# A decoder layer on one core: the softmax maximum moves into a spare row of the queries, and the transposed mask becomes one matmul per pair of heads

## The chip, the core and the metric

The kernel runs on one core of one Trainium2 chip. The metric is the device time of one execution in microseconds (us), the median of several runs. The core has five engines that run their own instruction streams and meet at semaphores: TensorE (PE in the profile), VectorE (DVE), ScalarE (ACT), GpSimd (POOL) and SyncE (SP), which here only issues transfers.

## The reference, cut to what matters

The layer takes x of 16 x 256 tokens with 128 features. It adds a selective-scan mixer, then a cross attention to 64 context keys per batch row, then a mixture of 8 experts with the best two chosen per token. The change is in the cross attention alone:

```
qh, kh, vh = heads of (q @ w_q.T + b_q), (k @ w_k.T + b_k), (v @ w_v.T + b_v)   # 16 heads of 8
score = einsum('bhqd,bhkd->bhqk', qh, kh) / sqrt(8)
score = where(mask == 0, -1e9, score)          # mask depends on query and key alone
attn  = softmax(score, axis=-1)                # subtracts each row's maximum
out   = einsum('bhqk,bhkd->bhqd', attn, vh) @ w_o.T + b_o
```

## The kernel before, in words

Two batch rows (512 tokens) are one unit of work; there are 8. The main loop has 8 rounds of 16 steps. In round r, step k, `body(r, k)` does one piece of the scan of unit r, and puts pieces of three other jobs between: the start of the mixer of units r+1 and r+2, the attention of unit r-1, and the end of the attention and the routing of unit r-2. What stands in which step is written out by hand in each engine's `slot` function, and each engine runs its list in that order. After the rounds, `drain` gives the attention of units 6 and 7 out between the 39 groups of the expert stage.

The scan in one step. ACT makes four decay tiles (`decays`, L1203) for the step three ahead, once VectorE's scan four steps back is done. DVE multiplies (`inputs`, L1711) and scans (`scan`, L1720). POOL multiplies (L1508) and folds (L1513) the states. PE sums them (`sum_states`, tile Y). The tiles lie in rings of four.

The attention of a unit has two passes over the scores. In the first (`scores`), queries lie on the partitions, and DVE takes each head's maximum over the 64 keys (`maxima`, L1737, steps 11 to 13). `split_max` (L1739) then makes minus the maximum as a sum of three bf16 numbers with five small DVE instructions. PE turns them (`turn_max`, L792), ACT copies them out of PSUM in one instruction (`copy_max`, L1254). In the second pass (`scores_t`, L798) keys lie on the partitions. To each product of keys and queries one bf16 matmul per pair of heads adds minus the maximum (`selmax` times `nmT`), and two more add the mask (`mbias2` times `identb`). ACT takes the exponential (`exps`, L1258).

Keys and queries are stored so that a contraction over 64 partitions serves one half of the heads. `qT` has two copies of the queries, w = 0 and 1, each with half of the 8-row head blocks set to zero (`queries`, L1119, by `qscale`). `Kbd` holds the keys four times, each with one head block kept in each group of 32 rows (`key_blocks`, L1243: four ACT instructions that scale `KT` by a column).

Three hand-overs stand near the change. `copy_xh` (ACT, L1207) at step 15 fills a PSUM tile that `steps_x` (DVE, L1693) multiplies at once. In step 6 ACT has one long block: `copy_kv`, `spreads`, `copy_xh`, `key_blocks`, `att_square`, `silus`, `att_inverse_root` (its last instruction is L1117). `att_normed` (DVE, L1732, step 9) needs the result of that last one.

## Time and profile before

| what | value |
|---|---|
| median of 3 runs | 830.47 us (830.2 to 832.67) |
| profiled execution: time / span | 829.18 / 827.4 us |
| busy: PE / DVE / ACT / POOL | 685.5 / 683.8 / 522.6 / 619.2 us |
| instructions: PE / DVE / ACT / POOL | 3923 / 1041 / 1223 / 467 |
| rounds of the scan | about 26 to 600 us of the span |
| `scores_t` pass, bf16 matmuls: `nmT,selmax` / `identb,mbias` | 128 / 256 |
| `Kbd` instructions on ACT | 32 |

The profiled execution took 829.18 us, of which the span, from its first to its last instruction, is 827.4. Busy time is summed per engine. A row of the timeline gives start and duration in us, the engine, the source line, the output and input tiles, the count of merged instructions, and in brackets how long the engine stood idle before and who released it. A row of `PE L649` is any matmul made through the helper at L649, so its tiles say which it is. The end of one instruction may overlap the start of the next on the same engine by about 0.1 us.

### The profile page before, as it was taken

To read this page: it belongs to the slowest core of one execution; us is meant where nothing else is said; L and a number is where in the kernel's file an instruction comes from. 1 tells how busy PE (TensorE), PEld (TensorE's weight loads), DVE (VectorE), ACT (ScalarE), POOL (GpSimd) and SP (SyncE) were. 2 spreads that over 40 slices of the span, in tenths; PEclk is the share of its full clock that TensorE was granted. 3 is DMA by queue.
4 is the path that set the end of the run, shared out by engine and by line. 5 is a ranking of instruction groups with operands and counts; after the bars stand their busy time and mean duration, and the time that the engine had idled before them with its cause. 6 is when DMAs were issued, how large, how long until landed. Compare 5 with 4: busy or idle time off the path is not lost. (4 is left out here: it accounts for less than half of the span.)

```text
span 827.4 us, 12371 instructions
## 1 busy us (share of the span) xinstructions
PE 685.5 (83%) x3923; PEld 477.2 (58%) x3923; DVE 683.8 (83%) x1041; ACT 522.6 (63%) x1223; POOL 619.2 (75%) x467
## 2 busy tenths in 40 slices
PE   6578759897898888889898798874778899899991
PEld 3453426555565555556555455552557678899981
DVE  3679999999999999999999999999953555865673
ACT  4687847787966977796697789567124334333353
POOL 1359988878899999999999999899752254675542
PEclk9679678999999999999999999989799999999997
DMA  4536595454538646534734644376064344886773
GB/s 106 205 116 163 183 280 183 127 202 161 156 125 225 211 152 199 169 130 128 228 136 154 190 158 154 109 237 211 27 211 127 97 139 128 268 294 219 230 257 102
DMA packets 80411, 142.70 MB, mean 172 GB/s; under 512 B 10555, under 2 KB 53574, under 8 KB 80346
## 3 DMA queue, kind: packets, MB, share of 16 engines
q1 hardware_dynamic: 75802, 133.38, 51.5%
q0 software_dynamic: 4544, 8.54, 2.9%
q8 instruction: 31, 0.51, 0.3%
q14 instruction: 34, 0.28, 0.1%
HBM read 110.25 MB, written 37.27 MB: 178 GB/s over the span
## 5 line engine op out<-in xcount | busy, mean ns | idle before, releaser
L1508 POOL TENSOR_TENSOR prod<-hst,BC 128x1024 f32<-128x1024 f32 x128 | 301.0, 2360 | 48.6 <-DVE hst L1720 40.0
L1720 DVE TENSOR_TENSOR_SCAN hst<-dA,Rp 128x1024 f32<-128x1024 f32 x128 | 292.3, 2284 | 9.0 <-ACT dA L1203 0.4
L1203 ACT ACTIVATE dA<-dtm,Aneg 128x255 f32<-128x255 f32 x512 | 213.9, 495 | 52.6 <-DVE hst L1720 52.0
L1513 POOL TENSOR_TENSOR prod<-prod 128x512 f32<-128x512 f32 x128 | 161.3, 1270 | 2.4
L1711 DVE TENSOR_TENSOR Rp<-BC,Rp 128x1024 f32<-128x1024 f32 x128 | 156.9, 1226 | 6.0 <-DMA BC<-bcd 0.6
L1628 POOL DMA_INDIRECT y2d<-prod,back x78 | 77.2, 990 | 101.6 <-DVE prod L2091 85.4
L649 PE MATMUL Y<-prod,ident 128*128 128x256 f32 x512 | 141.3, 409 | 14.3 <-POOL prod L1513 12.2
L649 PEld LDWEIGHTS Y<-prod,ident 128*128 128x128 f32 x512 | 101.4, 206 | 52.1 <-issue 19.1
L649 PE MATMUL Mb<-hpad,winT 128*128 128x512 f32 (+1 forms) x176 | 79.6, 598 | 14.5 <-ACT xh L1152 11.9
L649 PEld LDWEIGHTS Rp<-BC,xh 128*128 128x128 f32 x624 | 75.3, 192 | 7.7 <-ACT xh L1449 4.1
L649 PE MATMUL Rp<-BC,xh 128*128 128x128 f32 x624 | 76.4, 276 | 3.5 <-ACT xh L1449 3.5
L1552 POOL DMA_INDIRECT xsd<-x2o,slots x64 | 63.2, 987 | 17.5 <-issue 16.6
L649 PE MATMUL T<-Kbd,qT 64*128 64x256 f32 x256 | 50.2, 447 | 22.8 <-DVE mx L1737 19.7
L1442 ACT ACTIVATE soft<-Y 128x256 f32<-128x256 f32 x37 | 14.2, 384 | 83.9 <-PE Y L1045 83.9
L649 PEld LDWEIGHTS Mb<-hpad,winT 128*128 128x128 f32 x176 | 34.7, 205 | 51.5 <-issue 25.5
L649 PEld LDWEIGHTS T<-Kbd,qT 64*128 64x128 f32 x256 | 30.3, 204 | 41.7 <-DVE mx L1737 29.1
L1262 ACT ACTIVATE E<-T 128x512 f32<-128x512 f32 x64 | 34.7, 594 | 30.1 <-PE T L649 30.0
L649 PE MATMUL T<-qT,Kbd 64*128 64x256 f32 x256 | 37.2, 410 | 12.8 <-ACT E L1262 11.4
L1737 DVE TENSOR_REDUCE mx<-T 128x8 f32<-128x512 f32 x64 | 40.6, 676 | 6.7 <-PE T L649 6.7
L2085 DVE TENSOR_SCALAR xh<-Rp,BC 128x256 f32<-128x256 f32 x40 | 17.5, 478 | 26.6 <-PE Rp L649 26.6
L649 PE MATMUL Rp<-soft,BC 128*128 128x256 f32 x160 | 38.0, 380 | 1.2 <-ACT soft L1442 1.2
L649 PE MATMUL Mb<-soft,BC 128*128 128x256 f32 x152 | 36.2, 381 | 0.0
(282 smaller groups left out, 1127.0 us busy)
## 6 DMA issues: line engine op xcount, KB each, us to landing
BC<-bcd SPq DMA_DIRECT2D x63, 1024.0 KB, 5.4
BC<-recs SPq DMA_DIRECT2D x39, 578.0 KB, 4.2
xsd<-blank SPq DMA_DIRECT2D x17, 1056.0 KB, 11.9
dtm<-xsd SPq DMA_DIRECT2D x39, 132.0 KB, 4.1
recs<-in_L_ffn_W SPq DMA_DIRECT2D x16, 256.0 KB
...
```

Of the source, the lines that this page charges most:

```text
L649: return pe.matmul(o, l, r_, start=start, stop=stop, **kw)
L1203: m = A(dA[:, k % RING, i, 1:SEQ], dtm[:, r % 2, d, b * SEQ + 1:(b + 1) * SEQ], ACT.Exp, scale=Aneg[:, d, c * NC + i:c * NC + i + 1])
L1262: m = A(E[:, b, hp:hp + 3:2, :], T[h][:, :].rearrange("p (i s) -> p i s", i=2), ACT.Exp)
L1442: A(xg[:, j % 2, :], Turned[min(j, 2)], ACT.Copy).then_inc(s_xg, 1)
L1508: TT(prod[:, k % RING, :, :], hst[:, k % RING, :, :], BC[:, (k // 2) % BCR, 1, :, :], ALU.mult).then_inc(s_pd, 1)
L1513: TT(prod[:, k % RING, 0:NC // 2, :], prod[:, k % RING, 0:NC // 2, :], prod[:, k % RING, NC // 2:NC, :], ALU.add).then_inc(s_fd, 1)
L1552: pool.indirect_dma_start(out=xsd[:, :], out_offset=bass.IndirectOffsetOnAxis(ap=slots[:, c, t:t + 1], axis=0), in_=x2o[:, t, :], in_offse ...
L1628: pool.indirect_dma_start(out=y2d[:, :], out_offset=bass.IndirectOffsetOnAxis(ap=at, axis=0), in_=yr[:, j % YR, i, :], in_offset=None, bou ...
L1711: v.tensor_tensor(U, BC[:, (k // 2) % BCR, 0, :, :], DTX[:, d, :].unsqueeze(1).to_broadcast([P, NC, SEQ]), ALU.mult).then_inc(s_u, 1)
L1720: v.tensor_tensor_scan(hst[:, k % RING].rearrange("p n s -> p (n s)"), dA[:, k % RING].rearrange("p n s -> p (n s)"), U.rearrange("p n s - ...
L1737: v.tensor_reduce(mx[:, i, h * 8:h * 8 + 8], T[h][:, :].rearrange("p (h k) -> p h k", k=KEYS), AX.X, ALU.max).then_inc(Tv.sem, 1)
L2085: v.tensor_scalar(hid[:, j % 2, c, :], Up[j % 2][1][:, i, :], b1r[:, j % RINGS, c:c + 1], 0.0, ALU.add, ALU.max).then_inc(s_rb, 1)
```

## The change: what it does, and the diff

The maximum no longer goes through bf16 pieces. DVE writes each unit's maxima to columns of a wide tile `mx` whose other columns are zero. PE turns that tile in fp32. ACT copies four blocks of 32 rows of the result into the rows of `qT` that were zero: those of the other half of the heads. `Kbd` gets a second half (w = 0, 1), in which the rows that meet those rows of `qT` hold -1 for the right head. The product of keys and queries then already has the maximum subtracted. The first pass reads the swapped copy. `split_max`, `selmax`, `nm` and `nmT` go. The mask is turned once at the start into `mbiasT` and is added by one matmul per pair of heads, contracted over 64 rows.

```diff
         def _(pe):
...
-                        mm(T[h][:, w * SEQ:(w + 1) * SEQ], qT[rows, w, b, t * P:(t + 1) * P], Kbd[rows, b, :, :],
+                        mm(T[h][:, w * SEQ:(w + 1) * SEQ], qT[rows, 1 - w, b, t * P:(t + 1) * P], Kbd[rows, 1 - w, b, :, :],
...
             def turn_max(r):
-                pe.wait_ge(Tv.sem, Tv.at("me", r))
+                pe.wait_ge(Tv.sem, Tv.at("mx3b", r))
                 for i in range(NB * QT):
-                    m = pe.transpose(Tb[0:96, i * P:(i + 1) * P], nm[:, i, :, :], identb[:, :])
+                    m = pe.transpose(T[0][:, i * P:(i + 1) * P], mx[:, i, :], ident[:, :])
                 m.then_inc(Tp.sem, 1)
...
-                        mm(T[h][:, i * SEQ:(i + 1) * SEQ], Kbd[rows, b, 2 * g:2 * g + 2, :], qT[rows, i, b, :],
+                        mm(T[h][:, i * SEQ:(i + 1) * SEQ], Kbd[rows, i, b, 2 * g:2 * g + 2, :], qT[rows, i, b, :],
                            start=i == 0, stop=False, skip_group_check=True)
                 for i in range(2):
                     for h in range(2):
-                        o, hp = T[h][:, i * SEQ:(i + 1) * SEQ], TRIO[g][h][i]
-                        mm(o, selmax[:, hp, :], nmT[:, b * SEQ:(b + 1) * SEQ], start=False, stop=False, skip_group_check=True)
-                        for t in range(QT):
-                            m = mm(o[:, t * P:(t + 1) * P], mbias2[:, t, :, :], identb[:, :], start=False, stop=True,
-                                   skip_group_check=True)
+                        rows = slice(64 * h, 64 * h + 64)
+                        m = mm(T[h][:, i * SEQ:(i + 1) * SEQ], twice[rows, :, :], mbiasT[rows, :], start=False, stop=True,
+                               skip_group_check=True)
...
+            def turn_mask():
+
+                pe.wait_ge(s_k, 3)
+                pe.wait_ge(s_cT, 2)
+                for t in range(QT):
+                    m = pe.transpose(Tb[:, t * P:(t + 1) * P], mbias2[:, t, :, :], identb[:, :])
+                m.then_inc(s_mk, 1)
...
         def _(act):
...
+            def copy_mask():
+                act.wait_ge(s_mk, 1)
+                A(mbiasT[:, :], Tb[:, 0:SEQ], ACT.Copy).then_inc(s_mk, 1)
...
             def key_blocks(r):
...
-                for j in range(HP // 2):
-                    m = A(Kbd[:, :, j, :], KT[:, :, :], ACT.Copy, scale=blk4[:, j:j + 1])
+                for w in range(2):
+                    for j in range(HP // 2):
+                        m = A(Kbd[:, w, :, j, :], KT[:, :, :], ACT.Identity, bias=kshift[:, w, j:j + 1], scale=kscale[:, w, j:j + 1])
                 m.then_inc(s_kb, 1)

             def copy_max(r):
                 act.wait_ge(Tp.sem, Tp.at("m", r))
-                A(nmT[:, :], Tb[0:96, 0:NB * SEQ], ACT.Copy).then_inc(Ta.sem, 1)
+                for w in range(2):
+                    for h in range(2):
+                        rows = slice(64 * h + 32 * (1 - w), 64 * h + 32 * (2 - w))
+                        m = A(qT[rows, w, :, :].rearrange("p b s -> p (b s)"), T[0][rows, :], ACT.Copy)
+                m.then_inc(Ta.sem, 1)
...
         def _(v):
...
             def inputs(r, k):
-                if r and k == 14:
-                    v.wait_ge(Tv.sem, Tv.at("me", r - 1))
...
             def maxima(r, i):
...
-                    v.tensor_reduce(mx[:, i, h * 8:h * 8 + 8], T[h][:, :].rearrange("p (h k) -> p h k", k=KEYS), AX.X, ALU.max).then_inc(Tv.sem, 1)
+                    to = mx[:, i, 64 * h:64 * h + 64].rearrange("p (u x) -> p u x", u=2)[:, :, 0:HP // 2]
+                    v.tensor_reduce(to, T[h][:, :].rearrange("p (u j k) -> p u j k", u=2, k=KEYS), AX.X, ALU.max).then_inc(Tv.sem, 1)
-            def split_max(r):
...
-                v.tensor_scalar(part, mx[:, :, :], -1.0, None, ALU.mult).then_inc(Tv.sem, 1)
-                v.tensor_copy(nm[:, :, 0, 0:HEADS], part).then_inc(Tv.sem, 1)
-                v.tensor_tensor(part, part, nm[:, :, 0, 0:HEADS], ALU.subtract).then_inc(Tv.sem, 1)
-                v.tensor_copy(nm[:, :, 1, 0:HEADS], part).then_inc(Tv.sem, 1)
-                v.tensor_tensor(nm[:, :, 2, 0:HEADS], part, nm[:, :, 1, 0:HEADS], ALU.subtract).then_inc(Tv.sem, 1)
...
             def attention_scale():
...
+                for w in range(2):
+                    o = (1 - w) * GW
+                    nxt_(v.tensor_scalar(kscale[:, w, :], blk4[:, :], parity[:, w:w + 1], None, ALU.mult))
+                    nxt_(v.tensor_tensor(kshift[:, w, :], ident[:, o:o + HP // 2], ident[:, 64 + o:64 + o + HP // 2], ALU.add))
+                    nxt_(v.tensor_scalar(kshift[:, w, :], kshift[:, w, :], -1.0, None, ALU.mult))
```

On ACT, in round 3, steps 14 and 15, the list of the kernel before is the following; `nmT` is the copied maximum, `Rp<-xh` is `copy_xh`.

```order
L1203 ACTIVATE dA<-dtm,Aneg 128x255 x4
L1256 ACTIVATE nmT<-T 96x512
L1101 ACTIVATE rstd<-Mb,epsc 128x512
L1103 ACTIVATE rstd<-rstd 128x512
L1104 ACTIVATE sq<-Mb,epsc 128x512
L1106 ACTIVATE sq<-sq 128x512
L1262 ACTIVATE E<-T 128x2x256 x2
L1203 ACTIVATE dA<-dtm,Aneg 128x255 x4
L1214 ACTIVATE Rp<-xh 128x512
```

The same place of the changed kernel, on ACT:

```order
L1211 ACTIVATE dA<-dtm,Aneg 128x255 x4
L1272 ACTIVATE qT<-T 32x512 x4
L1109 ACTIVATE rstd<-Mb,epsc 128x512
L1111 ACTIVATE rstd<-rstd 128x512
L1112 ACTIVATE sq<-Mb,epsc 128x512
L1114 ACTIVATE sq<-sq 128x512
L1279 ACTIVATE E<-T 128x2x256 x2
L1211 ACTIVATE dA<-dtm,Aneg 128x255 x4
L1222 ACTIVATE Rp<-xh 128x512
```

One copy became four, and seven instructions and four decays stand behind them up to `copy_xh`. In step 6 of the same round, the long block of ACT before:

```order
L1214 ACTIVATE Rp<-xh 128x512
L1251 ACTIVATE Kbd<-KT,blk 128x2x64 x4
L1110 ACTIVATE sqt<-T,ncbo 128x512
L1152 ACT_TABLE_LOAD
L1152 ACTIVATE xh<-Mb,convb 128x512 x2
L1155 ACTIVATE sres<-Mb 128x512 x2
L1156 ACT_TABLE_LOAD
L1115 ACTIVATE rstdt<-T,epsc 128x512
L1117 ACTIVATE rstdt<-rstdt 128x512
```

And in the changed kernel, where `kshift` and `kscale` are the columns of the bias and the scale:

```order
L1222 ACTIVATE Rp<-xh 128x512
L1264 ACTIVATE Kbd<-KT,kshift,kscale 128x2x64 x8
L1118 ACTIVATE sqt<-T,ncbo 128x512
L1160 ACT_TABLE_LOAD
L1160 ACTIVATE xh<-Mb,convb 128x512 x2
L1163 ACTIVATE sres<-Mb 128x512 x2
L1164 ACT_TABLE_LOAD
L1123 ACTIVATE rstdt<-T,epsc 128x512
L1125 ACTIVATE rstdt<-rstdt 128x512
```

Four instructions that fill `Kbd` became eight, with a bias as well; nothing else in the block moved.

## Rows read from the trace of the kernel before

**Rows 1.** Busy time of each engine, step 13 of round 3 to that of 4

```profile
306.00:378.00 72.00, 62.71 (x359) 39.47 (x359) 69.68 (x78) 57.20 (x132) 67.70 (x48) 0.98 0.53 163
```

**Rows 2.** Groups on ACT by form: busy us, mean ns, idle before

```profile
L1251 ACT ACTIVATE Kbd<-KT,blk 128x128 f32<-128x128 f32 x32 | 10.1, 387 | 0.0
...
L1129 ACT ACTIVATE x1T<-T,bo 128x512 f32<-128x512 f32 x8 | 5.4, 678 | 0.8 <-PE T L649 0.8
...
L1256 ACT ACTIVATE nmT<-T 96x512 bf16<-96x512 bf16 x8 | 4.7, 593 | 22.1 <-PE T L795 22.1
...
L1142 ACT ACTIVATE xT<-Mb 128x512 f32<-128x512 f32 x8 | 4.6, 580 | 4.1 <-DMA lnb<-in_L_attn_ln_b 3.7 <-PE Mb L657 0.4
```

**Rows 3.** Timeline of DVE, round 3, steps 13 and 14

```profile
304.70 1.26 DVE L1737 TENSOR_REDUCE mx<-T 128x8 f32<-128x512 f32 x2
...
307.30 1.23 DVE L1711 TENSOR_TENSOR Rp<-BC,Rp 128x1024 f32<-128x1024 f32 x1
```

**Rows 4.** Timeline of PE: bf16 transposes, round 3, and fp32 ones, round 5

```profile
307.68 0.39 PE L795 MATMUL T<-identb,nm 128*96 128x128 bf16 x4
...
442.56 0.63 PE L657 MATMUL Mb<-ident,xin 128*128 128x128 f32 x4
```

**Rows 5.** Timeline of ACT, step 15 of round 1, steps 14 and 15 of round 3

```profile
171.41 0.59 ACT L1214 ACTIVATE Rp<-xh 128x512 f32<-128x512 f32 x1
...
308.10 0.59 ACT L1256 ACTIVATE nmT<-T 96x512 bf16<-96x512 bf16 x1 [0.72 <-PE T L795]
308.60 0.67 ACT L1101 ACTIVATE rstd<-Mb,epsc 128x512 f32<-128x512 f32 x1
...
313.65 0.59 ACT L1214 ACTIVATE Rp<-xh 128x512 f32<-128x512 f32 x1
```

**Rows 6.** Timeline of DVE, step 15 of rounds 1, 3 and 6

```profile
172.10 0.70 DVE L1693 TENSOR_TENSOR Rp<-dtm,Rp 128x512 f32<-128x512 f32 x1 [0.35 <-ACT Rp L1214]
...
314.46 0.67 DVE L1693 TENSOR_TENSOR Rp<-dtm,Rp 128x512 f32<-128x512 f32 x1
...
529.14 0.67 DVE L1693 TENSOR_TENSOR Rp<-dtm,Rp 128x512 f32<-128x512 f32 x1
```

**Rows 7.** Timeline of PE, round 6, step 13

```profile
522.00 0.42 PE L795 MATMUL T<-identb,nm 128*96 128x128 bf16 x4 [1.28 <-DVE nm L1752]
```

**Rows 8.** Timeline of ACT, round 3, from step 6

```profile
267.82 1.70 ACT L1203 ACTIVATE dA<-dtm,Aneg 128x255 f32<-128x255 f32 x4 [0.48 <-DVE hst L1720]
...
273.68 1.26 ACT L1251 ACTIVATE Kbd<-KT,blk 128x128 f32<-128x128 f32 x4
...
282.36 0.63 ACT L1117 ACTIVATE rstdt<-rstdt 128x512 f32<-128x512 f32 x1
```

**Rows 9.** Timeline of DVE, step 9 of rounds 3 and 5

```profile
283.05 0.73 DVE L1732 SCALAR_TENSOR_TENSOR sqt<-T,ncbo,rstdt 128x512 f32<-128x512 f32 x1
...
426.54 0.75 DVE L1732 SCALAR_TENSOR_TENSOR sqt<-T,ncbo,rstdt 128x512 f32<-128x512 f32 x1 [0.29 <-ACT rstdt L1117]
```

**Rows 10.** Timeline of ACT and DVE, round 1, step 9

```profile
140.21 0.63 ACT L1117 ACTIVATE rstdt<-rstdt 128x512 f32<-128x512 f32 x1
...
141.14 0.73 DVE L1732 SCALAR_TENSOR_TENSOR sqt<-T,ncbo,rstdt 128x512 f32<-128x512 f32 x1
```

**Rows 11.** Timeline of PE, second `scores_t` of unit 6; DVE, first expert groups

```profile
599.23 1.13 PE L649 MATMUL T<-qT,Kbd 64*128 64x256 f32 x8 [1.18 <-ACT E L1262]
600.29 0.28 PE L649 MATMUL T<-nmT,selmax 96*128 96x256 bf16 x1
...
601.21 1.08 PE L649 MATMUL Y<-prod,ident 128*128 128x256 f32 x4
...
611.80 0.22 DVE L2073 TENSOR_SCALAR late<-dtm,expert 128x2 f32<-128x2 f32 x1
```

**Rows 12.** Timeline of ACT and PE, attention of unit 7

```profile
640.82 1.26 ACT L1251 ACTIVATE Kbd<-KT,blk 128x128 f32<-128x128 f32 x4
...
664.70 0.42 PE L795 MATMUL T<-identb,nm 128*96 128x128 bf16 x4 [0.73 <-DVE nm L1752]
```

More of the change, by code:

```diff
@@ L100, in decoder @@
         mean = sb("mean", [P, P])
-        selmax = sb("selmax", [96, HP, P], BF16)
-        pickmax = sb("pickmax", [96, HEADS])
+        twice = sb("twice", [P, 2, KEYS], BF16)
         blk = sb("blk", [P, HEADS])
@@ L105, in decoder @@
         quads = sb("quads", [P, HP // 2])
+        parity = sb("parity", [P, 2])
+        kscale = sb("kscale", [P, 2, HP // 2])
+        kshift = sb("kshift", [P, 2, HP // 2])
         iota = sb("iota", [P, EXPERTS])
@@ L150, in decoder @@
         mbias2 = sb("mbias2", [P, QT, 2, KEYS], BF16)
+        mbiasT = sb("mbiasT", [P, SEQ], BF16)
         wgs = sb("wgs", [P, EXPERTS])
@@ L184, in decoder @@
         KT = sb("KT", [P, NB, KEYS])
-        Kbd = sb("Kbd", [P, NB, HP // 2, KEYS])
+        Kbd = sb("Kbd", [P, 2, NB, HP // 2, KEYS])
         Vg = sb("Vg", [P, NB, HP, GW])
@@ L193, in decoder @@
         rstdt = sb("rstdt", [P, TOK])
-        mx = sb("mx", [P, NB * QT, HEADS])
-        mpart = sb("mpart", [P, NB * QT, HEADS])
-        nm = sb("nm", [P, NB * QT, 3, 32], BF16)
-        nmT = sb("nmT", [96, NB * SEQ], BF16)
+        mx = sb("mx", [P, NB * QT, P])
         rden = rstdt
@@ L325, in decoder @@
         Ta = Marks(sem("Ta"), "KT V sq ln rs q m e00 e01 e10 e11 ld rd x2")
-        Tv = Marks(sem("Tv"), "xq " + " ".join(f"mx{i}a mx{i}b" for i in range(NB * QT)) + " ma mb mc md me n")
+        Tv = Marks(sem("Tv"), "xq " + " ".join(f"mx{i}a mx{i}b" for i in range(NB * QT)) + " n")
         s_kb = sem("s_kb")
+        s_mk = sem("s_mk")
         s_cT = sem("s_cT")
@@ L393, in decoder @@
             (alph[:, :], alpha.partition_broadcast(P)),
-            (pickmax[:, :], c_pickmax), (blk[:, :], c_blk), (iota[:, :], c_iota),
+            (blk[:, :], c_blk), (iota[:, :], c_iota),
             (att_nat[:, 0, :], w_q), (att_nat[:, 1, :], w_k), (att_nat[:, 2, :], w_v), (att_nat[:, 3, :], w_o),
@@ L414, in decoder @@
         MIXER = DT * TAPS // 4 + 2 + DT
-        NPRE = 1 + DT * TAPS + 7
+        NPRE = 1 + DT * TAPS + 8
         block = es.enter_context(nc.Block())
@@ L879, in slot @@
                         turn_contexts(k - 3)
+                    if k == 8:
+                        turn_mask()
                 if tail:
@@ L1248, in key_blocks @@
                 else:
-                    act.wait_ge(s_pre, NPRE + 6)
-                for j in range(HP // 2):
-                    m = A(Kbd[:, :, j, :], KT[:, :, :], ACT.Copy, scale=blk4[:, j:j + 1])
+                    act.wait_ge(s_pre, NPRE + 12)
+                for w in range(2):
+                    for j in range(HP // 2):
+                        m = A(Kbd[:, w, :, j, :], KT[:, :, :], ACT.Identity, bias=kshift[:, w, j:j + 1], scale=kscale[:, w, j:j + 1])
                 m.then_inc(s_kb, 1)
@@ L1316, in slot @@
                         copy_contexts(k - 4)
+                    if k == 9:
+                        copy_mask()
                 if tail:
@@ L1659, in _ @@
             v.memset(dA[:, :, :, 0:1], 0.0)
-            v.memset(nm[:, :, :, :], 0.0)
+            v.memset(mx[:, :, :], 0.0)
             v.memset(epsc[:, 0:1], EPS)
@@ L1868, in slot @@
                         maxima(r - 1, 3)
-                        split_max(r - 1)
                 if tail and k == 12:
@@ L1901, in drain @@
                         maxima(r - 1, k - 10)
-                    if k == 13:
-                        split_max(r - 1)
             v.wait_ge(s_first, FIRST)
@@ L1923, in _ @@
             nxt_(v.tensor_copy(identb[:, :], ident[:, :]))
-            nxt_(v.tensor_copy(selmax[:, :, :].rearrange("p g (h k) -> p (g h) k", h=2), pickmax[:, :].unsqueeze(2).to_broadcast([96, HEADS, KEYS])))
+            for h in range(2):
+                half = slice(64 * h, 64 * h + 64)
+                nxt_(v.tensor_copy(twice[half, :, :], ident[half, half].unsqueeze(1).to_broadcast([64, 2, KEYS])))
             v.wait_ge(s_prea, 1)
@@ L1942, in attention_scale @@
                 nxt_(v.tensor_reduce(quads[:, :], blk[:, :].rearrange("p (q j) -> p q j", j=HP // 2), AX.X, ALU.add))
-                nxt_(v.tensor_tensor(qscale[:, :], quads[:, 0:2], quads[:, 2:4], ALU.add))
-                nxt_(v.tensor_scalar(qscale[:, :], qscale[:, :], float(HD) ** -0.5, None, ALU.mult))
+                nxt_(v.tensor_tensor(parity[:, :], quads[:, 0:2], quads[:, 2:4], ALU.add))
+                nxt_(v.tensor_scalar(qscale[:, :], parity[:, :], float(HD) ** -0.5, None, ALU.mult))
                 nxt_(v.tensor_scalar(qbias[:, :], qscale[:, :], bq[:, 0:1], None, ALU.mult))
+                for w in range(2):
[3 more added lines that the diff above has]
+                    nxt_(v.tensor_scalar(kshift[:, w, :], kshift[:, w, :], -1.0, None, ALU.mult))
             def routing_constants(k):
```

9 lines of the change are left out of this document (removed).

## The prediction

> **What bounds the kernel now.** I read the busy time by slices and by rounds first. Through the rounds the clock granted to TensorE is full (0.98), and DVE is busy 69.68 of 72 us, more than any other engine [rows 1]. So a round lasts as long as DVE's list, and DVE time saved or waited for there moves the end. Behind about 600 us the chain of waits runs through matmuls: PE sets the end. Next I read the timelines of DVE and ACT side by side, asking at each place where DVE takes something from ACT how early ACT is. The average of 57.20 busy us on ACT [rows 1] does not answer that, and the list of waits shows nearly nothing, since a wait that ends just in time is no wait.
>
> **DVE: `split_max` goes.** The last maximum ends at 305.96 and the next multiply starts at 307.30 [rows 3]; without the five small instructions it would follow with the usual overlap of 0.08. That gives 1.42 us in each of rounds 1 to 7. In the first round the changed setup (six more DVE instructions of a few columns, two transposes, one copy) stands ahead of waits of DVE for ACT that are longer than it; I cost it at nothing, at most 1 us.
>
> **First hand-over, step 15.** The four bf16 transposes start at 307.68 in round 3, while the pieces are ready at about 307.27 (just ahead of the multiply at 307.30) [rows 3, 4]. PE comes to them from its own list, without a wait, in rounds 1 to 5, and that list hangs on the maxima of step 13, which do not move. So removing `split_max` does not start them earlier. In fp32 four transposes take 0.63 us where bf16 took 0.39 [rows 4]: +0.24. Then ACT copies. One copy of 96 partitions takes 593 ns and one of 128 takes 580 [rows 2], so partitions cost nothing and a copy of 32 rows costs the same. From one to the next ACT needs 0.50 (308.10 to 308.60) [rows 5], so four cost three times 0.49, +1.47. Everything behind on ACT is 1.71 late, down to `copy_xh`. That ended at 314.24 (313.65 and 0.59), and DVE took it at 314.46 [rows 5, 6]; with 0.10 for the hand-over (in round 1, where DVE waited, ACT ended at 172.00 and DVE started at 172.10 [rows 5, 6]) the margin is 0.12. DVE, 1.42 ahead by now, waits for it. What counts is the new time of `steps_x`: +1.71 in round 1, which waited already, and 1.71 - 0.12 = +1.59 in each of rounds 2 to 5. The gain of `split_max` is inside these numbers and is lost. Between copies and `copy_xh` ACT has the exponentials, whose scores PE has ready about 0.9 us earlier than needed, since `scores_t` is shorter, so they add no wait. In round 6 the four instructions of `inverse_roots_x` are absent and PE did wait 1.28 for the pieces [rows 7]; there the transposes move up by 1.28, the copies and the shorter `scores_t` leave the rest of ACT's list 0.45 earlier, and DVE meets `copy_xh` about 0.9 earlier than 529.14 [rows 6]. Sum: 1.71 + 4 x 1.59 - 0.9 = **+7.2**.
>
> **Second hand-over, step 9.** ACT's block of step 6 begins when DVE's scan of step 5 releases it (267.82, after 0.48 idle) and ends with 282.99 [rows 8]. DVE takes that result at 283.05 [rows 9], the earliest its own list allows. The gap of 0.06 has the hand-over itself in it, so the margin is between zero and 0.06; I take 0.02. In round 5 DVE waited, 0.29, so it is below zero [rows 9]. Into this block go the eight `Kbd` instructions. Before, four took 1.26 at 387 ns each [rows 2, 8], so one follows another after 0.29. The new ones have a bias column too; on 512 columns a bias costs 678 - 580 = 98 ns [rows 2], a duration of about 0.48, one each 0.38: 0.48 + 7 x 0.38 = 3.14, **+1.88** per unit. Only a wait of ACT behind them could hide this, and the ones there are for PE, which itself waits for the Silu of this block. So DVE is later by 1.86 in rounds 2, 3, 4, 6, by 1.88 in round 5, and in round 1, where ACT ends at 140.84 and DVE starts at 141.14 [rows 10], by 1.88 - 0.26 = 1.62. In round 7 the block has no Silus and no table loads, is far shorter, and costs DVE nothing. Sum: **+10.9**. No trace shows the new form at 128 columns: if the bias were free it would be 4 x 0.29 = +1.16 per unit and 6.6 over the rounds; if the eight did not overlap at all, 8 x 0.48 - 1.26 = +2.55 and 14.9. I take the middle, since the bias price is read from two rows of one kind.
>
> [...]
>
> **The tail.** Unit 6 (about 592 to 614 us): transposes 1.30 earlier, +0.4 for fp32 (at the lower clock after an idle PE), copies +1.47. Each `scores_t` had 1.06 of fp32 products and then 0.92 of bf16 [rows 11]. Four matmuls of 256 columns take the place of the latter. Eight fp32 ones of that size took 1.06, two halves of the rows at a time, so four take about 0.23 in bf16, by half that in one row half after the other 0.45; I take 0.23, -0.69 each, and twice that for the first, at half clock. Together 0.57 - 1.3 - 2.07 = -2.8. But PE's next work needs DVE's second tile, done at about 611.8 [rows 11]. I book **-2.4**. Unit 7: PE was held 0.73 at its transposes [rows 12], which start 0.87 earlier; +0.24, +1.47, 4 x -0.69 give -1.9. Against it, its `Kbd` block at 640.82 [rows 12] stands right ahead of an expert's ReLU that PE waits for: +1.85. Together **-0.1**.
>
> [...]
>
> **Sum.** 7.2 + 10.9 - 2.4 - 0.1 = +15.6, on 829.18 for the profiled execution: 844.8. The median of the runs stands 1.3 above that execution, so I expect **846**.
>
> **Rivals.** (1) Faster: ACT's extra work is hidden, because ACT has 15 idle us a round. Then 6 x 1.42 = 8.5 goes in the rounds, and 2.4 + 1.9 in the tail: 817.7. It decides if the margins at L1693 and L1732 exceed 1.7 and 1.9 us. For it speaks ACT's busy share; against it both hand-overs, read at 0.12 and 0.02. Chance 0.05. (2) Only `Kbd` costs: the transposes do follow `split_max` up in rounds 1 to 5, by 1.3. Then the first hand-over is 1.71 - 1.3 = 0.4 in round 1, 0.3 in each of four, -0.9 in round 6, +0.7 in all, the total 9.1: 839.6. Against it: no wait at 307.68. Chance 0.08. (3) More than forecast: PE, held longer for the Silu of step 6, also holds the sums that POOL needs, and DVE waits for POOL. POOL is busy 67.70 of 72 [rows 1], so 1 us a round over five rounds is possible: 851. Against it: DVE grows slower, which gives POOL room. Chance 0.07. (4) Bias free or nearly: 6.6 for 10.9 and 1.2 for 1.85, 841. Chance 0.08, a variant of my case. Mine, between 842 and 849: 0.72.
>
> **Chances and range.** This kernel's measurement can tell about 0.3%, 2.5 us, from no change. Faster is rival 1 and half as much again for what I don't see: 0.07. The same: 0.03, a case in which one hand-over costs what the other gives. Slower: 0.90. The range takes in the bounds 841 and 850 and reaches to rival 2: 838 to 850.
>
> **What would show it.** In the changed profile: DVE waits of about 3 us at `steps_x` for ACT's `Rp<-xh` in rounds 1 to 5, and of about 1.9 at `sqt<-T,ncbo,rstdt` in rounds 1 to 6; `Kbd` instructions of about 480 ns, four `qT` copies of about 580; transposes at the same distance from the last maximum as before in rounds 1 to 5; rounds of about 75 us in place of 71.5; from 600 us on about 2.5 us less than before. I am wrong if DVE's busy share in the rounds stays at 0.97, or if `Kbd` takes less than 2 us.

## The result, and the profile after

The changed kernel takes 858.24 us (median of 4 runs, 856.99 to 859.71), the one before 830.34 beside it (828.36 to 832.67). The ratio is 1.0326, 95% interval 1.0306 to 1.0347. The forecast was 846, range 838 to 850: the direction was right, the size was 15.6 where 27.9 was measured, outside the range. The profiled execution after took 856.99, with a span of 854.9 (before 827.4, so 27.5 more).

First the busy time of one round of the changed kernel, step 0 of round 4 to that of round 5 (columns as in [rows 1]):

```profile
331.00:407.00 76.00, 60.93 (x324) 37.46 (x324) 68.06 (x71) 59.88 (x138) 67.00 (x48) 0.96 0.51 154
```

DVE was busy 69.68 of 72 us [rows 1] and now is 68.06 of 76: it has less to do and waits for nearly 8 us. The clock is 0.96, where it was 0.98. Which waits these are is in the groups on DVE (the last number is the idle time ahead of the group, over all rounds):

```profile
L1712 DVE TENSOR_TENSOR Rp<-dtm,Rp 128x512 f32<-128x512 f32 x16 | 10.9, 683 | 18.0 <-ACT Rp L1222 18.0
...
L1749 DVE SCALAR_TENSOR_TENSOR sqt<-T,ncbo,rstdt 128x512 f32<-128x512 f32 x8 | 6.0, 747 | 19.1 <-ACT rstdt L1125 19.1
```

`steps_x` waited 1.2 us before and waits 18.0 now, `att_normed` 3.1 before and 19.1 now (of which 2.8 is behind the rounds both times; in rounds 1 to 6 it is 0.3 and 16.3). The two groups on ACT that grew (compare [rows 2]): `Kbd` 479 ns each (387 before, and twice as many), the `qT` copies of 32 rows 588 ns each.

```profile
L1264 ACT ACTIVATE Kbd<-KT,kshift,kscale 128x128 f32<-128x128 f32 x64 | 25.4, 479 | 0.0
...
L1272 ACT ACTIVATE qT<-T 32x512 f32<-32x512 f32 x32 | 18.8, 588 | 20.4 <-PE T L795 20.1
```

Here is the first hand-over in the timelines of round 3, to be compared with [rows 5, 6]. ACT:

```profile
322.70 2.39 ACT L1272 ACTIVATE qT<-T 32x512 f32<-32x512 f32 x4 [0.93 <-PE T L795]
325.11 0.69 ACT L1109 ACTIVATE rstd<-Mb,epsc 128x512 f32<-128x512 f32 x1
...
328.56 1.69 ACT L1211 ACTIVATE dA<-dtm,Aneg 128x255 f32<-128x255 f32 x4
330.15 0.59 ACT L1222 ACTIVATE Rp<-xh 128x512 f32<-128x512 f32 x1
```

And DVE:

```profile
323.89 1.23 DVE L1728 TENSOR_TENSOR Rp<-BC,Rp 128x1024 f32<-128x1024 f32 x1
325.21 2.29 DVE L1737 TENSOR_TENSOR_SCAN hst<-dA,Rp 128x1024 f32<-128x1024 f32 x1
330.85 0.70 DVE L1712 TENSOR_TENSOR Rp<-dtm,Rp 128x512 f32<-128x512 f32 x1 [3.35 <-ACT Rp L1222]
```

The buffer that `copy_xh` writes is free at 325.11, with DVE's multiply; the copies end there too; but `copy_xh` starts at 330.15, behind ten other instructions (four of `inverse_roots_x`, two exponentials, four decays; it was counted as eleven ahead of the prediction). Four copies take 2.41 us to the next instruction, 0.60 each, not the 0.49 that the forecast took for all but the last.

Here is the second hand-over in round 3. The forecast's point was that PE waits for the Silu of this block. The profile shows each fp32 product as two matmuls, so the two products of `gate_in` are the row with x4. PE before, then PE now:

```profile
277.71 1.99 PE L649 MATMUL Mb<-hpad,winT 128*128 128x512 f32 x4 [1.76 <-ACT xh L1152]
```

```profile
281.62 3.60 PE L649 MATMUL Mb<-hpad,winT 128*128 128x512 f32 x8
289.31 3.67 PE L649 MATMUL Mb<-hpad,winT 128*128 128x512 f32 x4 [4.09 <-ACT xh L1160]
```

On ACT:

```profile
283.37 3.17 ACT L1264 ACTIVATE Kbd<-KT,kshift,kscale 128x128 f32<-128x128 f32 x8
...
288.57 1.27 ACT L1160 ACTIVATE xh<-Mb,convb 128x512 f32<-128x512 f32 x2
291.42 0.60 ACT L1163 ACTIVATE sres<-Mb 128x512 f32<-128x512 f32 x1 [1.58 <-PE Mb L649]
293.01 0.60 ACT L1163 ACTIVATE sres<-Mb 128x512 f32<-128x512 f32 x1 [0.99 <-PE Mb L649]
```

And the busy times by stretch (the first number behind POOL's is the granted clock):

```profile
280.00:288.00 8.00, 5.22 (x17) 2.73 (x15) 7.78 (x7) 7.76 (x23) 7.92 (x7) 1.00 0.46 159
288.00:290.00 2.00, 0.69 (x1) 0.50 (x2) 1.90 (x2) 1.83 (x3) 2.00 (x2) 0.83 0.00 0
290.00:292.00 2.00, 2.00 (x3) 0.66 (x2) 1.91 (x2) 0.58 (x1) 2.00 (x2) 0.50 0.50 172
292.00:294.00 2.00, 2.00 (x6) 1.01 (x5) 0.83 (x1) 0.99 (x3) 0.40 (x2) 0.82 1.04 246
```

`Kbd` takes 3.17 us, as forecast (3.14). But PE, idle for 4.09 us for want of `xh`, runs the four matmuls of `gate_in` at a lower clock (0.50 from 290 to 292 us) and needs 3.67 us; before, behind a wait of 1.76, it needed 1.99. Before the wait the clock was full (1.00 from 280 to 288 us). ACT's `sres` Silus wait for them (0.64 and 0.26 before; 1.58 and 0.99 now), and DVE waits for ACT. In round 5 PE waited 3.35, kept the full clock (1.00 from 440 to 447 us), and `gate_in` took 1.98 us.

**Ledger, after less before, by the starts of the same instructions** (in us, the forecast in brackets). Setup +0.2 (0). First hand-over in rounds 1 to 6, the gain of `split_max` inside it: +2.1, four times +2.04, -0.65, together +9.6 (+7.2). Second: +1.67, 3.22, 3.59, 3.09, 1.91, 3.01, together +16.5 (+10.9). Other waits of DVE for PE in the rounds +2.5 (0). Unit 6 +0.5 (-2.4). Unit 7 -1.8 (-0.1). Sum +27.5 (+15.6). The ledger is of one execution of each kernel.

### The profile page after: what moved, and what is told of

It is laid out like the page before. It is cut to its first block and busy times, and to the rows that moved or that the text cites. A ratio compares the mean times of both kernels' runs of the same rounds, so it can differ in the third digit from the quotient of the medians.

```text
span 854.9 us, 11880 instructions
## 1 busy us (share of the span) xinstructions
PE 676.3 (79%) x3669; PEld 466.4 (55%) x3669; DVE 677.4 (79%) x1008; ACT 551.4 (65%) x1280; POOL 618.9 (72%) x467
## 5 line engine op out<-in xcount | busy, mean ns | idle before, releaser
L649 PE MATMUL Y<-prod,ident 128*128 128x256 f32 x512 | 145.1, 418 | 17.1 <-POOL prod L1532 13.7
L1647 POOL DMA_INDIRECT y2d<-prod,back x78 | 77.2, 989 | 100.0 <-DVE prod L2098 83.8
L649 PEld LDWEIGHTS Y<-prod,ident 128*128 128x128 f32 x512 | 103.5, 209 | 57.4 <-issue 22.9
L649 PE MATMUL Mb<-hpad,winT 128*128 128x512 f32 (+1 forms) x176 | 86.1, 640 | 23.9 <-ACT xh L1160 22.5
L649 PEld LDWEIGHTS Mb<-hpad,winT 128*128 128x128 f32 x176 | 37.3, 219 | 62.6 <-ACT xh L1160 31.0
L649 PE MATMUL T<-qT,Kbd 64*128 64x256 f32 x256 | 39.7, 432 | 33.4 <-ACT E L1279 18.7
L649 PEld LDWEIGHTS T<-qT,Kbd 64*128 64x128 f32 x256 | 24.0, 202 | 47.1 <-ACT E L1279 25.7
```

Source lines behind the costliest of these rows:

```text
L649: return pe.matmul(o, l, r_, start=start, stop=stop, **kw)
L1647: pool.indirect_dma_start(out=y2d[:, :], out_offset=bass.IndirectOffsetOnAxis(ap=at, axis=0), in_=yr[:, j % YR, i, :], in_offset=None, bou ...
```

## Experiments

All ratios are to the kernel before, run beside each kernel (its medians there 831.3 to 832.4), with 95% intervals. Spans of single executions differ by some 4 us before round 1 begins: `steps_x` of round 1 starts between 101.7 and 106.1 us in kernels with nearly the same setup. So medians are compared, and below them the lengths of rounds (from one start of the first `steps_x` of a unit to that of the next). The rows are of one profiled execution of each kernel, which is not always near the median; where it is off by more than 2 us, its time stands with it.

**`copy_xh` right behind the copies.**

```
                 if prev and k == 14:
                     copy_max(r - 1)
+                    if r + 1 < ROUNDS:
+                        copy_xh(r + 1, 0)
...
-                if k == 15 and r + 1 < ROUNDS:
+                if k == 15 and r == 0:
                     copy_xh(r + 1, 0)
```

> The changed kernel, with ACT's `copy_xh` for the next round moved ahead: right behind the four `qT` copies of `copy_max`, in front of the four instructions of `inverse_roots_x`, the first exponentials and the decays of step 15. It can start there: DVE's multiply of step 15, which frees its buffer, ends at 325.11 in round 3, just as the copies do. Theory: the first hand-over costs only what stands between the copies and `copy_xh` in ACT's list. DVE's waits at `steps_x` (3.90, four times 3.35, 0.68, 18.0 in all) go, since the copy now ends at about 325.7 and DVE's scan of step 15 at 327.5: 858.2 - 18.0 = 840.2, or 842 if other waits give 0.3 a round back. Rival: the time comes back at step 9 or at DVE's waits for PE, because the rest of ACT's and PE's lists is as late as before; then half of it at most is gained, 849.

Measured: 839.59 us, 1.0092 (1.0063 to 1.0121), 18.6 less than the changed kernel. All of DVE's wait at `steps_x` is gone in rounds 1 to 6, 18.0 in all. So the place in ACT's list was the whole of that wait. The 18.6 are not this wait alone: in the profiled execution (841.68) DVE's waits at `att_normed` fell too, from 16.3 to 11.1, and a new one appears in rounds 3 to 6, 0.9 to 1.1 a round for POOL's `nl` (the input of DVE's `least`). ACT and DVE in round 3:

```profile
315.88 2.39 ACT L1272 ACTIVATE qT<-T 32x512 f32<-32x512 f32 x4 [0.93 <-PE T L795]
318.33 0.60 ACT L1222 ACTIVATE Rp<-xh 128x512 f32<-128x512 f32 x1
```

```profile
318.39 2.29 DVE L1739 TENSOR_TENSOR_SCAN hst<-dA,Rp 128x1024 f32<-128x1024 f32 x1
320.59 0.67 DVE L1714 TENSOR_TENSOR Rp<-dtm,Rp 128x512 f32<-128x512 f32 x1
```

**`Kbd` between the Silus.**

```
-            def silus(r):
+            def silus(r, keys=None):
...
+                if keys is not None:
+                    key_blocks(keys)
                 for d in range(DT):
                     act.wait_ge(Ap.sem, Ap.at(f"rs{d}", r))
```

> The changed kernel, with the eight `Kbd` instructions (3.17 us) moved from ahead of `att_square` and the Silus to between the Silus of `xh` and those of `sres`. PE then gets `xh` 3.17 earlier. Theory: the second hand-over cost more than the 1.88 forecast because PE, idle for 4.09 instead of 1.76 us, ran the four matmuls of `gate_in` at the lower clock (3.67 us instead of 1.99 in round 3). Here they run at full clock while ACT makes `Kbd`, and the waits of the `sres` Silus for PE (0.64 and 0.26 before the change) are covered by `Kbd` too. ACT's block ends 2.6 earlier in rounds 2, 3, 4 and 6 and 0.9 earlier in rounds 1 and 5: 12.2 less, 846; DVE's waits at `sqt<-T,ncbo,rstdt` near 1.0. Rival: PE's clock has no part in it, and only the 0.9 of covered waits is gained in each of six rounds: 5.4 less, 853.

Measured: 848.22 us, 1.0182 (1.0154 to 1.0210), 10.0 less than the changed kernel. `gate_in` took 1.99 us after a wait of 0.98, and DVE waited 0.61 at `att_normed` in rounds 3 to 6, better than expected. Part of it was given back at step 13, where DVE waited 1.0 a round for PE's counts (`places`) in rounds 2 to 6; the changed kernel has such a wait in rounds 3 and 5 alone. By the clock PE had dropped to the lower level there (0.50 from 378 to 386 us), behind its waits for `qT` and the maxima. That this drop makes the wait was not tested in this kernel. The rows are of round 4 of an execution of 855.20; the other four took 844.9 to 849.2.

```profile
374.00:376.00 2.00, 0.97 (x4) 0.17 (x2) 1.85 (x15) 2.00 (x5) 1.05 (x3) 1.00 0.05 12
376.00:378.00 2.00, 2.00 (x10) 1.04 (x10) 2.00 (x3) 1.94 (x3) 2.00 (x2) 0.62 0.00 0
378.00:380.00 2.00, 0.61 (x2) 0.00 (x0) 2.00 (x3) 2.00 (x4) 2.00 (x2) 0.50 0.04 14
380.00:386.00 6.00, 5.98 (x16) 4.26 (x17) 6.00 (x6) 6.00 (x16) 6.00 (x5) 0.50 0.53 178
```

**PE filled ahead of `gate_in`.**

```
                         conv(r + 1, 1)
+                        if prev:
+                            pe.wait_ge(Ta.sem, Ta.at("V", r - 1))
+                            for _ in range(3):
+                                mm(T[1][:, :], ident[:, :], attT[:, :, :])
                         gate_in(r + 1)
```

> The changed kernel, with three extra fp32 products of 512 columns (about 2.7 us, into a free bank, their result unused) on PE between the convolution and `gate_in` in rounds 1 to 6, where PE waits up to 4.09 us for ACT's `xh`. Nothing else moves. Theory: the clock falls because PE idles there. With the products the idle stretch is 1.4 us, `gate_in` takes 1.99 us in every round, the Silus of `sres` wait 0.6 and 0.3 again in place of 1.58 and 0.99, and DVE's wait at `sqt<-T,ncbo,rstdt` is 2 to 2.2 in every round: 1.3 to 1.7 less in rounds 2, 3, 4 and 6, 5.5 in all, 852.7. Rival: the clock falls for another reason, or DVE's extra wait there has another; then the time stays at 858, and above it if the products hold PE up.

Measured: 850.93 us, 1.0226 (1.0199 to 1.0253): 7.3 less than the changed kernel, for work that nobody uses. PE in round 3 (the three unused products are the row with x6):

```profile
286.88 2.73 PE L649 MATMUL T<-attT,ident 128*128 128x512 f32 x6
290.40 1.98 PE L649 MATMUL Mb<-hpad,winT 128*128 128x512 f32 x4 [0.78 <-ACT xh L1164]
```

`gate_in` is back at 1.98 us, and DVE's wait at `att_normed` is 1.56, 2.20, 2.20, 1.80, 1.79, 1.80 in rounds 1 to 6, 11.4 in all where the changed kernel has 16.3. Rounds 4 and 5 take 75.10 us each (76.3 and 77.2 in the changed kernel): at full clock they have the length of the forecast, "about 75". The gain over the expected 5.5 is for the most part in waits for PE's counts: the 0.97 of round 3 and the 0.46 and 1.06 of round 5 are gone. The profiled execution (854.55) is the slowest of four: its rounds 1 to 6 are 8.7 shorter than those of the changed kernel, but 2.6 of it are lost ahead of round 1, as in other kernels, and 3.7 behind the rounds, which was not followed up.

**Only the keys, in the kernel before.**

```
-                for j in range(HP // 2):
-                    m = A(Kbd[:, :, j, :], KT[:, :, :], ACT.Copy, scale=blk4[:, j:j + 1])
+                for to in (Kx, Kbd):
+                    for j in range(HP // 2):
+                        m = A(to[:, :, j, :], KT[:, :, :], ACT.Identity, bias=zeros[:, j:j + 1], scale=blk4[:, j:j + 1])
```

> The kernel before, with one thing added: `key_blocks` makes eight instructions with a scale and a bias column each (four of them into an unused tile) in place of four with a scale alone; the maxima, `split_max` and `scores_t` are the old ones. ACT's block of step 6 grows by 1.9 us in rounds 1 to 6. Theory: this alone makes the whole second hand-over. DVE waits at `sqt<-T,ncbo,rstdt`, 10.9 in all by the forecast's term, and since PE idles longer before `gate_in` and its clock falls, 1.2 to 1.7 more in about four rounds: 830.3 + 10.9 + 5.5 = 846.7. Rival: in this kernel the clock holds (PE's other work stands otherwise), and the cost is the forecast's 10.9: 841.3. Third: ACT's spare time hides it, 830.

Measured: 852.13 us, 1.0262 (1.0232 to 1.0293), 20.8 more than before: twice the forecast's term, and 4 more than this expectation. The waits at `att_normed` are 1.56, 3.38, 2.60, 3.99, 2.63, 2.19, together 16.4 (0.3 before); waits for PE's counts make 3.9 more in rounds 2 to 6, where the kernel before has none. Round 4 shows the clock at its worst (0.50 from 361 to 366 us), on PE:

```profile
361.69 3.78 PE L651 MATMUL Mb<-hpad,winT 128*128 128x512 f32 x4 [3.35 <-ACT xh L1154]
```

The wait here is 3.35, as in round 5 of the changed kernel, where the clock held and `gate_in` took 1.98. The length of one wait alone doesn't tell what the next matmuls get.

**Only more copies, in the kernel before**, of 32 rows each, and of 96 partitions each.

```
+                for n in range(3):
+                    A(nmx[32 * n:32 * n + 32, :], Tb[32 * n:32 * n + 32, 0:NB * SEQ], ACT.Copy)
                 A(nmT[:, :], Tb[0:96, 0:NB * SEQ], ACT.Copy).then_inc(Ta.sem, 1)
```

> The kernel before, with one thing added: `copy_max` makes three more copies of 32 rows and 512 columns (rows 0, 32 and 64 on, into an unused tile) ahead of its own copy. `Kbd`, `split_max`, the transposes and `scores_t` are the old ones. Theory: copies whose range of partitions changes from one to the next do not overlap; each takes 0.60 to the next one's start, as in the changed kernel, and ACT's list to `copy_xh` is 1.8 longer: DVE waits 0.35 + 1.8 in round 1 and about 1.7 in each of rounds 2 to 5, nothing in round 6, about 2 more in the tail: 830.3 + 1.8 + 6.8 + 2 = 841. Rival: one starts 0.49 after the other, as the full ones do, and the time is 830.3 + 1.5 + 5.5 + 1.5 = 839. Third: if DVE's waits behind them hide it, 830.

The other one has `A(nmx[n][:, :], Tb[0:96, 0:NB * SEQ], ACT.Copy)` in the loop.

> As the kernel with the three added copies of 32 rows, but each of the three copies 96 partitions, rows 0 to 95, into a tile of its own. Theory (what breaks the overlap is the change of the range of partitions): one starts 0.49 after the other, ACT's list is 1.5 longer, and DVE waits 0.3 a round less at `steps_x` than with the 32-row copies: 839. Rival (the cost does not depend on it): the same pitch and the same time as with 32-row copies, 841 if that is 0.60.

Measured: 848.11 us, 1.0191 (1.0165 to 1.0217) with 32 rows; 845.09 us, 1.0142 (1.0107 to 1.0178) with 96. On ACT, 32 rows:

```profile
315.08 1.78 ACT L1258 ACTIVATE nmx<-T 32x512 f32<-32x512 bf16 x3 [0.72 <-PE T L796]
316.87 0.59 ACT L1259 ACTIVATE nmT<-T 96x512 bf16<-96x512 bf16 x1
```

96 partitions:

```profile
313.07 1.56 ACT L1258 ACTIVATE nmx<-T 96x512 f32<-96x512 bf16 x3 [0.72 <-PE T L796]
314.52 0.60 ACT L1259 ACTIVATE nmT<-T 96x512 bf16<-96x512 bf16 x1
```

One copy follows another after 0.60 where each has its own range of 32 rows and after 0.48 where it is the same 96 rows. DVE's waits at `steps_x` in rounds 2 to 5 are 1.57 and 1.22 (the second in an execution of 848.06). So the price that was taken for a copy holds. The reason, that the range changes, is not shown: the number of rows changed as well, and no run copies the same 32 rows again and again. It is not just any change of range, for the copy of rows 0 to 95 and the instruction on all 128 rows behind it do overlap (0.50 from start to start, [rows 5]). Both times are 6 to 7 above the expectations, though. With 32 rows the profiled span is 19.0 longer than before: 1.5 ahead of round 1, 11.8 in the rounds (expected 8.6; round 6 waits 1.11, where nothing was expected, and 1.4 are waits for PE's counts), and 5.7 behind them, where 2 were expected. That last part was not followed up.

**Both moves.**

> The changed kernel with both moves: `copy_xh` right behind the `qT` copies, and the `Kbd` instructions between the Silus. Alone they gave 18.6 and 10.0 (858.2 to 839.6 and to 848.2). Theory: the two hand-overs are the whole loss and stand at different places, so the gains add: 829.6, no wait at `steps_x`, 0.6 to 1 at `sqt<-T,ncbo,rstdt`. Rival: DVE, no longer stopped at step 15, meets ACT and PE later in their lists at step 9 and at the scores, the clock falls there, and a third of the second gain is lost: 833 to 836.

Measured: 828.18 us, 0.9959 (0.9934 to 0.9984). The gains add (858.2 less 18.6 and 10.0 is 829.6), and this form beats the kernel before by a little. From round 3 on rounds take 71.3 to 71.5 us (the profiled execution took 831.30); DVE waits 0.9 to 1.1 for POOL's `nl` and 0.5 at `att_normed` in each.

**First move and filled PE** (`copy_xh` first, and the unused products ahead of `gate_in`).

> The changed kernel with `copy_xh` right behind the `qT` copies (839.6 alone) and the three unused products on PE ahead of `gate_in` (850.9 alone, from 858.2). Theory: `gate_in` took 1.98, 2.58, 3.13, 3.46, 1.98 us in rounds 1 to 5 with the first edit alone; at full clock it takes 1.98 in each, and DVE's waits at `sqt<-T,ncbo,rstdt` (11.1 in rounds 1 to 6) fall by about 4, if they are 1.3 to 1.6 each: 835.5. Rival: what remains there is ACT's longer list alone and PE's clock is not behind it: 839.6, or more, since the products hold PE up by up to 0.4 a round.

Measured: 831.44 us, 1.0001 (0.9990 to 1.0011): 8.2 less than the first move alone, twice what was expected, and the rival is wrong. DVE's waits at `att_normed` in rounds 1 to 6 fell from 11.1 to 6.6, and these rounds are 5.5 shorter in all; the rest of the 8.2 stands outside them and was not followed up. So with the first hand-over mended, unused products on PE bring the kernel back to the time of the kernel before.

**First move and `Kbd` at step 8**, and the same **with `least` a step later**.

```
                 if prev and k == 6:
-                    key_blocks(r - 1)
                     att_square(r - 1)
...
                 if prev and k == 8:
+                    key_blocks(r - 1)
                     queries(r - 1)
```

> The changed kernel with `copy_xh` right behind the `qT` copies, and the eight `Kbd` instructions moved out of ACT's block of step 6 altogether, to step 8, right ahead of `queries`. ACT's block is then 1.26 us shorter than in the kernel before, and 3.17 shorter than in the changed one; behind it ACT waited 0.7 for PE's product for the queries, and DVE takes the scores 1.7 after PE has them, so 3.17 there is 1.2 later than before and fits. Theory: no wait of DVE for ACT is left in rounds 2 to 6; what is left is DVE's wait of 0.93 for POOL's `nl`, seen as soon as `copy_xh` was early. That is 0.55 a round less than with `Kbd` between the Silus (828.2): 825. Rival: the scores come late, or PE's clock falls in the longer wait for them, and the time is 830 or more.

> As the kernel with `copy_xh` first and `Kbd` at step 8, and in addition DVE's `least` (the minimum over `nl`) one step later, at step 8. Theory: DVE's wait of 0.93 for POOL at `least` was a bound of its own in rounds 3 to 6; POOL has that result long before step 8, and ACT needs `least` only behind its block. 4 to 5 times 0.9 less: 821. Rival: POOL, busy 67.7 us of a round, is the bound now in another place, or DVE's wait turns up at `sqt<-T,ncbo,rstdt`, and the time stays at 825.

Measured: 831.66 us, 1.0007 (0.9990 to 1.0023), and 830.70 us, 0.9981 (0.9962 to 1.0000). Neither gain came. The rival of the first holds, scores that come late. The second rival named the right outcome, no gain, but not the place: DVE's wait at `att_normed` is gone, and with the second edit the one for POOL too, and DVE waits for PE's scores instead, 0.7 to 2.0 in nearly every round. PE waited 3.28 us for `qT` and soon ran at the lower clock: the first scores behind the wait took 1.13, the second 2.67, and the clock was 0.50 from 366 to 370 us. PE in round 4 of the kernel with both edits, then the stretches:

```profile
362.98 1.13 PE L649 MATMUL T<-Kbd,qT 64*128 64x256 f32 x8 [3.28 <-ACT qT L1130]
...
365.27 2.67 PE L649 MATMUL T<-Kbd,qT 64*128 64x256 f32 x8 [0.36 <-DVE mx L1757]
```

```profile
362.00:366.00 4.00, 2.67 (x13) 1.51 (x14) 3.33 (x4) 3.94 (x6) 4.00 (x3) 0.78 0.27 86
366.00:370.00 4.00, 4.00 (x14) 2.62 (x13) 4.00 (x3) 4.00 (x12) 4.00 (x4) 0.50 0.53 176
```

**The same (with `least` later), with PE filled ahead of the scores.**

```
                     if k == 9:
+                        for _ in range(3):
+                            mm(T[0][:, :], ident[:, :], attT[:, :, :])
                         scores(r - 1, 0)
```

> As the kernel with `copy_xh` first, `Kbd` at step 8 and `least` a step later (830.7), with three unused fp32 products of 512 columns (2.6 us) on PE right ahead of the scores of step 9, where PE waits 3.3 us for the `qT` of `queries`. Theory: what keeps that kernel from 821 is PE's clock alone: behind the wait it stands at 0.50 from 366 to 370 us, the second scores take 2.67 instead of 1.13, and DVE waits 0.7 to 2.0 a round at its maxima and 0.2 to 0.6 for PE's counts. With the products the clock holds, and about 1.5 a round goes over rounds 2 to 6: 823. Rival: the scores are late because ACT makes `Kbd` there, and DVE waits for them at any clock: 829 to 831.

Measured: 825.00 us, 0.9923 (0.9903 to 0.9943), the fastest of all: 5.7 less than without the products, where 7.7 was expected. At this second place too, the clock is up with unused products (1.00 in both stretches, 0.78 and 0.50 without), and the kernel is faster. PE and the same stretches:

```profile
356.02 2.74 PE L649 MATMUL T<-attT,ident 128*128 128x512 f32 x6
359.47 1.13 PE L649 MATMUL T<-Kbd,qT 64*128 64x256 f32 x8 [0.71 <-ACT qT L1132]
...
361.70 1.73 PE L649 MATMUL T<-Kbd,qT 64*128 64x256 f32 x8 [0.57 <-DVE mx L1759]
```

```profile
362.00:366.00 4.00, 4.00 (x30) 2.87 (x29) 4.00 (x4) 4.00 (x11) 4.00 (x3) 1.00 0.58 223
366.00:370.00 4.00, 3.08 (x17) 1.97 (x16) 3.93 (x9) 4.00 (x12) 4.00 (x5) 1.00 0.61 224
```

Rounds 3 to 6 take 70.4 to 70.6 us, against 71.3 to 72.1 without the products, and the waits for scores there are 0.5 to 0.8. The runs of this kernel spread more than others, 819.3 to 830.9, and the rows are of the fastest (819.30), so these differences overstate the gain between medians.

**Controls.** The products ahead of `gate_in` in the kernel before:

> The kernel before with the three unused products on PE ahead of `gate_in`, as a control. There `gate_in` already runs in 1.98 us in all rounds, behind waits of 0.49 to 2.19 us. Theory (the products help only where the clock had fallen): no gain; 2.6 us of products in waits of 1.5 to 2.2 hold `gate_in` up by 0.4 to 1.1 a round, part of it visible since DVE's margin at `sqt<-T,ncbo,rstdt` is near zero: 830 to 835. Rival: busy PE raises the clock in other stretches too (the granted clock is 0.51 from 294 to 296 us), and the kernel before gains as the changed one did: 825.

Measured: 837.32 us, 1.0051 (1.0025 to 1.0078). Where the clock had not fallen ahead of `gate_in`, the products bring nothing. What they cost is less clear: the ten runs spread from 831.2 to 839.2, and in the profiled one (833.09) rounds 1 to 6 are only 1.6 longer than before. So the sign of the difference is measured, its size and cause are not.

The mask alone (the kernel before, with the mask added by one product over 64 rows):

> The kernel before with the second half of the change alone: the mask enters `scores_t` as one product of 256 columns with `twice` and `mbiasT` in place of two of 128 with `identb`; maxima, `split_max`, `nmT` with `selmax` and `Kbd` are the old ones. Theory: PE is not what DVE waits for in the rounds, so nothing there moves; in the tail each of eight `scores_t` has 0.92 us of bf16 products, about 0.45 of it the old mask, and gets it for 0.23: about 0.2 each, 1.5 in all: 829. Rival: the alternation between 64 rows and 96 or 128 rows costs PE something each time and this form, with more of it in a row, saves 0.5 per call: 826. Third: the extra setup (two transposes, a copy, two DVE instructions) costs as much as is saved: 830.3.

Measured: 832.71 us, 1.0017 (0.9999 to 1.0035). The new mask by itself gains nothing that can be measured: the interval leaves out the theory's -1.5 and the rival's -4, and the third answer, no change, stands. The trace shows why a `scores_t` hardly gets shorter. Here is one of unit 7 (the clock was 1.00 in both places), with the mask alone and then in the changed kernel:

```profile
669.36 1.13 PE L652 MATMUL T<-qT,Kbd 64*128 64x256 f32 x8 [0.68 <-ACT nmT L1275]
670.43 0.61 PE L652 MATMUL T<-nmT,selmax 96*128 96x256 bf16 x4
670.97 0.39 PE L652 MATMUL T<-mbiasT,twice 64*128 64x256 bf16 x4
```

```profile
696.11 1.14 PE L649 MATMUL T<-qT,Kbd 64*128 64x256 f32 x8 [2.48 <-ACT qT L1272]
697.08 0.39 PE L649 MATMUL T<-mbiasT,twice 64*128 64x256 bf16 x4
```

From start to start, the fp32 products take 1.07 where 96-row products follow and 0.97 where 64-row ones do, and the 96-row products take 0.54 ahead of 64-row ones, where four of them among 128-row ones take about 0.46 (half of the 0.91 from 666.87 to 667.78 in the kernel before). So each change of the number of rows goes with 0.08 to 0.10 us here, whatever its reason. With the mask alone there are two more changes per call, and they take back most of what the shorter mask gives: the call takes 1.93 us, to the next product's start at 671.29, where it took 1.97 before.

And `least` later in the form with both moves:

> The fastest form so far (`copy_xh` first, `Kbd` between the Silus, 828.2) with DVE's `least` one step later, so that its wait of 0.93 for POOL goes. Theory: ACT's block of step 6, released by DVE's scan of step 5, is the longer path to `sqt<-T,ncbo,rstdt`; DVE only waits there instead, 0.55 + 0.93 = 1.48 a round, and the time stays at 828. Rival: the wait for POOL was of its own and 0.93 a round goes over rounds 3 to 7: 824.

Measured: 828.34 us, 0.9958 (0.9942 to 0.9974). DVE's wait for POOL goes, and 1.47 stands at `att_normed` in rounds 4 to 6, where 1.48 was expected: ACT's block is the longer path there.

```profile
356.68 0.75 DVE L1754 SCALAR_TENSOR_TENSOR sqt<-T,ncbo,rstdt 128x512 f32<-128x512 f32 x1 [1.47 <-ACT rstdt L1125]
```

## Why the prediction was right in direction and wrong in size

**`split_max` goes: right.** The steps between the maxima and step 15 are 1.43 shorter in each round (forecast 1.42), and all of it is lost at `steps_x` in rounds 1 to 5. Rival 2, transposes that follow up, did not happen. They start 1.71 behind the last maximum (320.34), as they did 1.72 behind it before (305.96):

```profile
319.08 1.26 DVE L1755 TENSOR_REDUCE mx<-T 128x8 f32<-128x512 f32 x2
```

```profile
322.06 0.60 PE L795 MATMUL T<-ident,mx 128*128 128x128 f32 x4
```

**First hand-over: mechanism right, one size off.** DVE waits at `steps_x` in rounds 1 to 6, as said, and the move of `copy_xh` gives back 18.6. So rival 1, in which ACT's idle time hides the extra work, is out. The step that was mis-sized is "From one to the next ACT needs 0.50 (308.10 to 308.60) [rows 5], so four cost three times 0.49". Those two instructions, on 96 and on 128 rows, overlap; the new copies, on four ranges of 32 rows, do not and follow one another after 0.60. The ledger has +9.6 for +7.2: 0.45 in each of rounds 2 to 5, the rest in rounds 1 and 6.

**Second hand-over: the step that failed.** The block's own growth was right (each `Kbd` instruction took 479 ns, all eight 3.17 us for 3.14; in rounds 1 and 5, where the clock held, +1.67 and +1.91 for +1.62 and +1.88). So rival 4 (bias free) is out. What failed is "Only a wait of ACT behind them could hide this, and the ones there are for PE, which itself waits for the Silu of this block". That counted PE's part as a fixed duration moved later. PE's wait grew from 1.76 to 4.09 in round 3, its next matmuls ran wholly or in part at half the clock in rounds 2, 3, 4 and 6 (2.90 to 3.67 us for 1.98), and DVE was 1.2 to 1.7 later than forecast each time: +5.6 in all. The filled PE shows it: nothing else was changed, `gate_in` returned to 1.98 us, and 7.3 us went. Not all of the excess is the clock's: with the products DVE still waits 2.20 at `att_normed` in rounds 2 and 3, for 1.86 forecast; there the products may hold `gate_in` up themselves. The forecast named the clock only for the tail. Rival 3 (PE held longer, 851) had the engine right but the path wrong. POOL did wait more for PE's sums, 30.6 us over the span where it waited 7.6, but DVE did not wait for POOL in rounds 1 to 6; the lateness came back through ACT.

**Waits for PE elsewhere, +2.5, not in the forecast.** 0.42 in round 2, 0.97 in round 3, 0.46 and 1.06 in round 5, for PE's counts: 2.9, less 0.4 for small waits of the kernel before that are gone. In the run with the filled PE those of rounds 3 and 5 are gone and round 2 keeps its 0.42. So those of rounds 3 and 5 hang on PE's clock as well, and the one of round 2 stays open.

**The tail.** Unit 7 gained 1.8 where 0.1 was forecast: each `scores_t` is 0.69 shorter, as worked out (665.81 to 667.78 before, 696.11 to 697.39 after). A gain beyond that, for a change in the number of rows saved, is not there: the new call has none inside, but the 128-row products behind it now follow 64-row ones. By the size of the gain, the +1.85 for `Kbd` did not reach the end; that was not tested. Unit 6 lost 0.5 instead of gaining 2.4. Its PE timeline:

```profile
621.41 0.66 PE L795 MATMUL T<-ident,mx 128*128 128x128 f32 x4 [0.84 <-DVE mx L1755]
624.54 2.08 PE L649 MATMUL T<-qT,Kbd 64*128 64x256 f32 x8 [2.48 <-ACT qT L1272]
626.41 0.64 PE L649 MATMUL T<-mbiasT,twice 64*128 64x256 bf16 x4
628.22 2.08 PE L649 MATMUL T<-qT,Kbd 64*128 64x256 f32 x8 [1.18 <-ACT E L1279]
```

PE waits 2.48 for the four copies (0.68 for one before), and now the second `scores_t` too runs at the lower clock (0.50 from 624 to 632 us): 2.08 for its fp32 products, where it had 1.13 [rows 11]. The forecast gave half clock to the first alone, which had taken 2.00 before (594.31).

**Signs and range.** Of the signs that were named, the waits at `steps_x` (3.35 to 3.90), the two durations on ACT and the transposes came as said; the waits at `att_normed` (up to 3.48 for 1.9), the rounds (73.5 to 77.9 us for 75) and the tail (1.3 shorter behind the first hand-over of round 6, for 2.5) did not. The range reached to 850, the bound without overlap of `Kbd`; rival 3 was just outside. In the rounds, no case had PE's clock as a cost. That one cause stands behind most of the 12 us that were missed (5.6, at least 2.0 of the 2.5, and a part of unit 6's 2.9); 2.4 come for the most part from a price read from the wrong pair of rows.
